# Expert rows: store by slot and gather twice, or add into x3 by an indirect DMA

## The reference

```
logits = z3 @ router_w                       # 4096 x 8
gate_vals, idx = top_k(logits, 2)            # two of eight experts for each row
gates = softmax(gate_vals)
out = 0
for e in range(8):
    h = relu(z3 @ w1[e] + b1[e]) @ w2[e] + b2[e]
    y = layernorm(z3 + h, gamma[e], beta[e])
    w = sum(where(idx == e, gates, 0))
    out = out + w[:, None] * y
return x3 + out
```

## Time and profile before

| | |
|---|---|
| median of 3 runs | 3586.35 us (3580.56 to 3590.44) |
| the profiled execution | 3575.87 us, span 3574.1 us |
| mean granted TensorE clock | 0.897 |
| slot loop, from its first to its last residual add | 3125.4 to 3457.4 us |
| the rest, to the end of the span | 3457.4 to 3574.1 us |

### The profile page before, as it was taken

How to read it: one execution, slowest core, us unless ns; L and a number is a source line. 1 busy time by engine, 2 the same in 40 slices (tenths; PEclk the granted TensorE clock), 3 DMA queues, 4 the chain that set the end, 5 groups by cost and what they waited for, 6 DMA issues and landing times. The chain is left out here.

```text
span 3574.1 us, 57773 instructions
## 1 busy us (share of the span) xinstructions
PE 2822.7 (79%) x12010; PEld 1811.5 (51%) x12011; DVE 2576.7 (72%) x5150; ACT 1472.9 (41%) x4642; POOL 2200.7 (62%) x2242
## 2 busy tenths in 40 slices
PE   7898888844888888887888887866999997599960
PEld 5555555522333333334655555645787785366630
DVE  6766666625899999998888887885656552477764
ACT  6322322213565556665545454533333332144420
POOL 2477777776777777776777777752222210088866
PEclk9788888867999999998999999987999999799985
DMA  3444444444777777776777777774222222633339
GB/s 108 170 161 142 148 157 136 150 142 151 210 208 210 209 209 210 209 209 185 214 214 213 213 210 215 212 227 152 79 73 83 73 71 95 215 109 112 112 120 320
DMA packets 234218, 594.77 MB, mean 166 GB/s; under 512 B 50865, under 2 KB 59954, under 8 KB 229170
## 3 DMA queue, kind: packets, MB, share of 16 engines
q0 software_dynamic: 127104, 362.93, 35.9%
q1 hardware_dynamic: 102898, 222.79, 17.7%
q10 hardware_dynamic: 4032, 7.34, 0.6%
HBM read 500.74 MB, written 92.15 MB: 166 GB/s over the span
## 5 line engine op out<-in xcount | busy, mean ns | idle before, releaser
L1214 PE MATMUL at_bank<-product,v_hot 128*128 128x260 f32 x2432 | 629.8, 404 | 117.8 <-DVE product L970 110.9
L1168 PE MATMUL at_bank<-wide,hot_t 128*128 x1216 | 614.1, 627 | 124.6 <-ACT hot_t L1036 65.5
L803 POOL DMA_INDIRECT fetched<-t_k,at_index x608 | 581.7, 957 | 192.5 <-issue 133.7
L812 POOL DMA_INDIRECT fetched<-t_v,at_index x608 | 577.2, 949 | 197.0 <-issue 133.1
L348 POOL DMA_INDIRECT records<-staged,address x544 | 533.1, 980 | 265.0 <-issue 165.3
L1214 PEld LDWEIGHTS at_bank<-product,v_hot 128*128 128x128 f32 x2432 | 443.1, 195 | 299.0 <-issue 136.1
L886 DVE TENSOR_TENSOR product<-at_bank,fetched 128x512 f32<-128x512 f32 x608 | 413.7, 682 | 52.4 <-issue 33.6
L970 DVE TENSOR_TENSOR product<-fetched,at_turn 128x520 f32<-128x520 f32 x608 | 405.8, 689 | 62.3 <-DMA fetched<-t_v,at_index 31.2
L1168 PEld LDWEIGHTS at_bank<-wide,hot_t 128*128 128x128 f32 x1216 | 206.6, 194 | 377.7 <-issue 332.0
L617 PE MATMUL qkv_prod<-wide 128*128 128x512 f32 x768 | 378.0, 653 | 0.0
L843 DVE TENSOR_REDUCE raw_score<-product 128x7 f32<-128x448 f32 x608 | 348.2, 575 | 0.0
(11 more groups left out here) (292 smaller groups left out, 4330.2 us busy)
## 6 DMA issues: line engine op xcount, KB each, us to landing
row_bc<-in_src SPq DMA_DIRECT2D x34, 1024.0 KB, 4.7
by_slot<-m_y SPq DMA_DIRECT2D x72, 256.0 KB, 2.0
low_bc<-low_row SPq DMA_DIRECT2D x34, 512.0 KB, 5.5
fetched<-t_k,at_index POOLq DMA_INDIRECT x608, 3.7
fetched<-t_v,at_index POOLq DMA_INDIRECT x608, 3.8
records<-staged,address POOLq DMA_INDIRECT x544, 2.1
t_v<-wide SPq DMA_DIRECT2D x32, 260.0 KB
wide<-in_x SPq DMA_DIRECT2D x32, 256.0 KB, 2.9
```

Source lines behind the costliest of these rows:

```text
L803: eng.indirect_dma_start(fetched[:, n % SLOTS, 0:C], None, k, bass.IndirectOffsetOnAxis(index[:, t:t + 1], 0)).then_inc(s_row[n % SLOTS], 16)
L812: eng.indirect_dma_start(fetched[:, n % SLOTS, :], None, v, bass.IndirectOffsetOnAxis(index[:, t:t + 1], 0)).then_inc(s_row[n % SLOTS], 16)
L1168: nc.tensor.matmul(q_edge[u % 4][:, :], hot_t[:, g % 2, u % BATCH * P:(u % BATCH + 1) * P], q_sb[:, bass.ds(at, 1), :].rearrange("p a c -> ...
L1214: last = nc.tensor.matmul(bank[g % 2 * 2 + n][:, 0:HALF], hot[:, u % 4, :], product[:, u % 4, n * HALF:(n + 1) * HALF], start=first, stop= ...
```

## The change

Each expert's tile is multiplied by its gates and added in DRAM to the rows of x3 by an indirect DMA with an add. When all is added, x3 is copied to the output. In parts:

- `by_slot`, `acc`, the 64 gathers, the loads of x3, the 64 multiply-adds and the stores of the sum are gone. SP waits for the last adds and issues 16 copies, DRAM to DRAM, of 256 rows each.
- The add of slot u-1 is issued by GpSimd at the end of slot u, from `y`, and waits until the add of slot u-2 has landed, since two tiles can hold the same row. Its indices are copied once in four slots (`put_index`).
- GpSimd's multiplication by gamma goes. VectorE does (y - mean) * gamma and then * root + beta, in two instructions of three operands in place of L2031 and L2037.
- ScalarE multiplies by the gate (`weigh`). The gate comes with the gathered row: z3 gets 8 more columns, one for each expert, and 128 rows of zeros ahead of it, for empty places. x3 gets 128 spare rows ahead of it as well. An empty place p names spare row p.
- SP stores the zero rows and the gates (4096 pieces of 32 bytes) to z3; GpSimd waits for both ahead of the first gather. VectorE makes the table of gates ahead of the lists.

```
-            def store(i, more):
-                for u in range(TURN):
-                    e_done.wait(eng, i, u)
-                    eng.dma_start(tile_rows(by_slot, i, TURN, u), y[:, u % 4, :]).then_inc(e_put.sem(u), 16)
...
+            eng.wait_ge(s_blank, 1)
+            eng.dma_start(z3[0:P, :], blank_row[:, :]).then_inc(s_gates_put, 16)
+            eng.wait_ge(s_gates, 1)
+            eng.dma_start(z3_gates, gate_of[:, 0, :, :]).then_inc(s_gates_put, 16)
+            for u in range(TURN - PUTS, TURN):
+                wait_put(eng, TURNS - 1, u)
+            for n in range(PARTS):
+                mine = slice(n * (NODES // PARTS), (n + 1) * (NODES // PARTS))
+                eng.dma_start(out[mine, :], x3[P:, :][mine, :]).then_inc(s_out, 16)
+            eng.wait_ge(s_out, 16 * PARTS)
...
+            def scatter(i, u):
+                half = u // HALF
+                wait_put(eng, i, u - 1)
+                if u % HALF == 0:
+                    eng.sem_inc(s_passed, 1)
+                    eng.tensor_copy(put_index[:, half, :], row_of[:, bass.ds(i * TURN + half * HALF, HALF)]
+                                    ).then_inc(e_put_index.sem(half), 1)
+                    e_put_index.wait(eng, i, half)
+                e_done.wait(eng, i, u)
+                eng.sem_inc(s_passed, 1)
+                eng.indirect_dma_start(x3, bass.IndirectOffsetOnAxis(put_index[:, half, u % HALF:u % HALF + 1], 0),
+                                       y[:, u % PUTS, :], None, compute_op=ALU.add).then_inc(put[u % PUTS], 16)
...
                     if u < TURN - 1 or more:
                         residual(i, u + 1)
-                    e = expert(eng, i, u)
-                    e_norm.wait(eng, i, u)
-                    eng.tensor_tensor(y[:, u % 4, :], y[:, u % 4, :], flat(gamma_sb[:, e, :]),
-                                      ALU.mult).then_inc(e_gain.sem(u), 1)
+                    if u:
+                        scatter(i, u - 1)
+                scatter(i, TURN - 1)
...
+            def weigh(i, u):
+                e = eng.value_load(expert_of[0:1, bass.ds(i * TURN + u, 1)], min_val=0, max_val=E - 1)
+                e_norm.wait(eng, i, u)
+                mine = y[:, u % PUTS, :]
+                nc.scalar.activation(mine, mine, ACT.Copy, scale=rows_sb[:, u, bass.ds(e + C, 1)]
+                                     ).then_inc(e_done.sem(u), 1)
...
                         hidden(i, u + 1)
                         hidden_columns(i, u + 1)
+                    if u:
+                        weigh(i, u - 1)
                     e_var.wait(eng, i, u)
                     nc.scalar.activation(root[:, :], mean_var[:, 1:2], ACT.Sqrt, bias=eps[:, :]).then_inc(e_root.sem(u), 1)
...
-                e_put.wait(eng, i, u - 4)
+                wait_put(eng, i, u - PUTS)
...
-                per.link(nc.vector.reciprocal(root[:, :], root[:, :]))
-                nc.vector.tensor_scalar(mine, mine, mean_var[:, 0:1], root[:, :], ALU.subtract, ALU.mult
-                                        ).then_inc(e_norm.sem(u), 1)
+                nc.vector.reciprocal(root[:, :], root[:, :])
+                per.link(nc.vector.scalar_tensor_tensor(mine, mine, mean_var[:, 0:1], flat(gamma_sb[:, e, :]),
+                                                        ALU.subtract, ALU.mult))
+                nc.vector.scalar_tensor_tensor(mine, mine, root[:, :], flat(beta_sb[:, e, :]), ALU.mult, ALU.add
+                                               ).then_inc(e_norm.sem(u), 1)
```

More of the change, by code:

```diff
@@ L1616, in _, with experts @@
             turns(begin, body, lambda t, c: (up(t), down(t, 0), down(t, 1)), eng)
-def experts(nc, moved, count, x3, z3, router, w1, b1, w2, b2, gamma, beta, by_slot, out):
+def experts(nc, moved, count, x3, z3, router, w1, b1, w2, b2, gamma, beta, out):
     EPS = 1e-6
@@ L1663, in experts @@
         row_id = sb("row_id", [P, T])
+        to_spare = sb("to_spare", [P, 1])
+        spare = sb("spare", [P, SLOTS])
         slot_at = sb("slot_at", [1, SLOTS])
-        rows_sb = sb("rows", [P, TURN, C])
+        blank_row = sb("blank_row", [P, C + E])
+        rows_sb = sb("rows", [P, TURN, C + E])
         zT = sb("zT", [P, 2, C])
@@ L1713, in experts @@
         s_both, s_counted, s_open, s_list, s_ready = (sem(n) for n in ("both", "counted", "open", "list", "ready"))
-        s_norm, s_passed, s_passed_v, s_passed_pe, s_sum = (sem(n) for n in ("norm", "passed", "passed_v", "passed_pe", "sum"))
+        s_norm, s_passed, s_passed_v, s_passed_pe = (sem(n) for n in ("norm", "passed", "passed_v", "passed_pe"))
+        s_gates, s_gates_put, s_blank, s_out = (sem(n) for n in ("gates", "gates_put", "blank", "out"))
         r_load = Ring([sem(f"load{b}") for b in range(TURN)], TURN, 16)
@@ L1723, in experts @@
         names = ("e_turn", "e_zT", "e_up", "e_h", "e_hturn", "e_hT", "e_down", "e_res", "e_y", "e_var", "e_root",
[L1724 to L1728, removed]
+                 "e_norm", "e_done")
+        (e_turn, e_zT, e_up, e_h, e_hturn, e_hT, e_down, e_res, e_y, e_var, e_root, e_norm, e_done) = (
+            Ring([sem(n)], TURN) for n in names)
+        e_index, e_put_index = (Ring([sem(n)], 2) for n in ("e_index", "e_put_index"))
         got = moved[16:16 + TURN]
-        got_y = moved[24:24 + TOP * HALF]
-        c_index, c_sum = Ring([sem("c_index")], 2), Ring([sem("c_sum")], HALF)
-        c_x3, c_out = (Ring([sem(f"{n}{b}") for b in range(HALF)], HALF, 16) for n in ("c_x3", "c_out"))
+        put = moved[16 + TURN:16 + TURN + PUTS]
         block = open_block(nc, ctx, used)
@@ L1738, in tile_rows, with wait_put @@
             return v[bass.ds(i * per + u, 1), :, :].rearrange("a p c -> (a p) c")
+        def wait_put(eng, i, u):
+            eng.wait_ge(put[u % PUTS], i * (16 * (TURN // PUTS)) + (count + 16 * (u // PUTS + 1)))
         def by_turn(eng, turns, body):
@@ L1789, in _ @@
+            for u in range(TURN - PUTS, TURN):
[4 more added lines that the diff above has]
+            eng.wait_ge(s_out, 16 * PARTS)
         @block.gpsimd
         def _(eng):
-            for r in (e_res, e_gain):
-                r.start(eng)
+            e_res.start(eng)
+            eng.memset(blank_row[:, :], 0.0).then_inc(s_blank, 1)
@@ L1815, in gather @@
                 e_res.wait(eng, i, u - TURN)
+                e_done.wait(eng, i, u - TURN)
                 eng.sem_inc(s_passed, 1)
@@ L1853, in _ @@
             by_turn(eng, TURNS, body)
[L1855 to L1872, removed]
         @block.scalar
         def _(eng):
-            for r in (r_zT, e_zT, e_h, e_hT):
+            for r in (r_zT, e_zT, e_h, e_hT, e_done):
                 r.start(eng)
-            eng.wait_ge(s_cut, 9)
+            eng.wait_ge(s_cut, 10)
             with eng.Fori(0, T // TURN) as i:
@@ L1922, in body @@
                         hidden_columns(i, u + 1)
+                    if u:
+                        weigh(i, u - 1)
                     e_var.wait(eng, i, u)
                     nc.scalar.activation(root[:, :], mean_var[:, 1:2], ACT.Sqrt, bias=eps[:, :]).then_inc(e_root.sem(u), 1)
+                weigh(i, TURN - 1)
             e_root.start(eng)
             by_turn(eng, TURNS, body)
[L1928 to L1931, removed]
         @block.vector
         def _(eng):
-            for r in (r_route_sb, r_kept, r_hot, e_y, e_var, e_norm, e_done, c_sum):
+            for r in (r_route_sb, r_kept, r_hot, e_y, e_var, e_norm):
                 r.start(eng)
@@ L1998, in _ @@
             st.link(nc.vector.tensor_tensor(gate[:, 1, :], gate[:, 0, :], ratio[:, :], ALU.mult))
+            st.link(nc.vector.tensor_tensor(gate_of[:, :, :, :], one[:, :, :, :],
+                                            gate[:, :, :].unsqueeze(3).broadcast_to([P, TOP, T, E]), ALU.mult))
+            nc.vector.tensor_tensor(gate_of[:, 0, :, :], gate_of[:, 0, :, :], gate_of[:, 1, :, :], ALU.add
+                                    ).then_inc(s_gates, 1)
             with eng.Fori(0, LIST_TURNS) as i:
@@ L2014, in _ @@
             eng.wait_ge(s_open, 2)
-            nc.vector.tensor_copy(row_of[:, :], list_ps).then_inc(s_ready, 1)
+            st.link(nc.vector.tensor_scalar(spare[:, :], list_ps, 0.0, to_spare[:, :], ALU.is_equal, ALU.mult))
+            nc.vector.scalar_tensor_tensor(row_of[:, :], list_ps, float(P - 1), spare[:, :], ALU.add, ALU.add
+                                           ).then_inc(s_ready, 1)
             eng.wait_ge(s_w, 96)
@@ L2042, in _ @@
                     norm(i, u)
[L2043 to L2053, removed]
-                                                            acc[:, u, :], ALU.mult, ALU.add))
-                    nc.vector.scalar_tensor_tensor(acc[:, u, :], rows_sb[:, u * TOP + 1, :], gate[:, 1, n],
-                                                   acc[:, u, :], ALU.mult, ALU.add).then_inc(c_sum.sem(u), 1)
         @block.tensor
```

55 lines of the change are left out of this document (23 added, 32 removed).

## The result

The changed kernel takes 3635.34 us (median of 4 runs, 3630.24 to 3647.68) against 3585.17 us; the ratio is 1.0145 (95% interval 1.0114 to 1.0175). It is 50 us slower where 75 us faster was forecast. The ratios in this document compare only the undisturbed executions of both kernels, the medians all of them. The profiled execution took 3647.68 us with a span of 3646.0 us.

What follows compares the result with a forecast made beforehand. TensorE and the ring of VectorE and GpSimd, nearly level, were taken to bound the loop, transfers the sum. Sum's removal -70, loop -7, start +1.5 on 3575.9 gave 3500 us, as median 3511; range 3480 to 3610.

Steps and rivals of the forecast that it cites:

- first two rivals: Loop: adds set the pace; first, L = 4.8, 3569 us, chance 0.17; second, up to L = 5.5, 3620 us, chance 0.20.
- second rival: Loop: adds so long that the loop eats the whole saving; at L = 5.5, +34 us, 3620 us, chance 0.20.
- turning point: Loop: the pace of 5.64 us a slot, L = 5.06, at which the loop eats the whole saving of 68.5 us.
- L: Loop and end: time from issue to landing of one indirect add to x3, taken as 4.0 us.
- the prediction's own formula: Loop: change is 71 x (pace - 4.68) us; the pace is the slowest of 4.4, 4.4 (TensorE) and L + 0.58.
- the pace of the chain of adds: Loop: each add waits for the previous landing; L plus gap 0.3 plus index copies 0.28, so 4.58 us a slot.
- The gap behind a landing: Loop: time ahead of each DMA on GpSimd, put at 0.3 us in the chain of adds.
- GpSimd's own pace: Loop: gather 1.00, residual 1.28, add issue 1.00, gaps and index copies: 4.4 us a slot; 4.9 with a dearer issue.
- costs nothing in the ordinary slot: Loop: port lock between VectorE's new instructions and GpSimd's residual; 0 in ordinary slots, up to 1.3 us with an index copy.
- the ring of VectorE and GpSimd: Loop: GpSimd at 4.69 us a slot, nearly level with TensorE's 4.4; relieving one gives 0.2 or 0.3 us at most.
- T: End: the last residual add, from which the end is counted; last add lands at T+10, kernel ends at T+47.
- The lower bound: End: the copy from DRAM to DRAM takes at least 29.9 us, as a load of 8192 KB; 36 was taken.

Runs made afterwards that it cites:

- e2: The changed kernel with a plain indirect store in place of the indirect add, all waits kept; loop 345.6 us, ratio 0.9880.
- e3: The changed kernel with each turn's last add and last weighing moved into the next turn's first slot; loop 411.4 us, ratio 1.0114.
- e6: e3's kernel with the index copy moved ahead of the wait for the add before; loop 401.5 us, ratio 1.0108 to the kernel before.
- e7: The edits of e3 and e1 together on the changed kernel, odd slots' part left out of the output; loop 363.7 us, ratio 0.9930.
- e1: The changed kernel with odd slots' adds to a second DRAM tensor, each add waiting for the one two slots before; loop 374.3 us, ratio 1.0032.
- e11: The kernel before with only the new normalising, e5's kernel on another chip; loop 298.7 us, 3548.26 us, ratio 0.9894.
- e5: The kernel before with gamma and beta in VectorE's two three-operand instructions, store by slot and sum kept; loop 298.9 us, ratio 0.9902.
- e8: The changed kernel with SP storing weighed rows by slot in place of GpSimd's add, experts' part left out of the output; loop 325.3 us, ratio 0.9836.
- e4: The kernel before with the sum replaced by the copy of x3, experts' part left out of the output; end 38.0 us for 116.7, ratio 0.9937.
- e12: e6's kernel timed again on the chip of e11, against the kernel before; loop 401.3 us, 3595.27 us, ratio 1.0025.

## Why the prediction was wrong

That the adds set the pace was in the forecast itself and in its first two rivals, at different lengths. By the sign the second rival came, with a chance of 0.20; by the length of an add it is not, since its turning point was put at L = 5.06, and L is 4.9. By the prediction's own formula the kernel should still have been some 10 us faster. So more than one step failed, and that a rival named the right sign is in part luck. The steps that failed are the pace of the chain of adds, put at L + 0.58 = 4.58 (points 1 and 2), and the ends of the turns, put at nothing (point 3).

1. **The length of an add** (the term of the sum that was mis-sized): L = 4.0 was taken between 3.5 and 5.5; 4.9 was measured. The base was right: an indirect store without the add was put at 2.7 and takes 2.9 to 3.2 (e2), 0.2 to 0.5 more. The add's own part was put at 1.3 and is 1.8. That is 0.9 x 71 = 64 us. The Trainium skill's rule of two reads for each write ("Collectives: The Full Stack", bandwidth ceiling), stated there for a ring of cores, gave 3.6 as an estimate; the measured add costs 1.8 us over the store, twice what doubling the 0.93 us of data would cost. The rule points the right way and is too small here.
2. **The gap behind a landing**: 0.3 was taken from DMAs issued back to back. Behind a wait it is 0.8 (e2, and the chain after). Those 0.5 us, 36 us in 71 slots, turn the sign once L is 4.9: 10 us faster become 26 slower. A row of issues that wait for nothing doesn't price an issue that waits.
3. **The ends of the turns** were not in the sum at all. The diff shows `scatter(i, TURN - 1)` behind the loop over u; the prediction treated every slot alike. 32 us (e3), the add's place and the weighing's together. With the three put right, and 0.14 us a slot for the index copies (e3 to e6), the formula gives 71 x (4.9 + 0.8 + 0.14 - 4.68) + 32 = 114 us for the loop; 112 were measured.
4. **GpSimd's own pace** was put at 4.4, with an add's issue at 1.0. It is 5.1 (e7), with 1.7 to 1.8 for the issue there and 1.6 in the kernel after. The upper bound named for it was 1.5.
5. **VectorE against GpSimd**: "costs nothing in the ordinary slot" held for a GpSimd that arrives when computed. In e1 and e7, where it has hardly a pause, the instruction with gamma takes 1.29 and 1.48 for 0.76, in the kernel after 0.90. The exclusive lock of the Trainium skill's "SBUF — State Buffer" fits.
6. **The new normalising** was worth nothing in the prediction, TensorE standing at 4.4 a slot. Alone it is worth 33 us. TensorE's 318 us of busy time were no floor: between the first and the last residual add the same number of its instructions was busy 308.7 us before and 292.9 in e11, which runs at 4.2 a slot. Busy time read in a loop that waits can be too long. The kernel before was bound by the ring of VectorE and GpSimd, and by more than 0.3 us.
7. **The end** came out at 47.2 for 47, with errors that cancel: the copy starts at T+17.7 for T+10, and takes 29.5 for 36. The later start comes from a third add still outstanding at T: they were issued at T+1.0, T+6.7 and T+12.9 (3599.82, 3605.49, 3611.74), where the sum had two, at T+1.7 and T+6.0. The lower bound, a load of the same size in 29.9 us, was the right row for a copy from DRAM to DRAM.
8. **The start**: +1.5 was right for the lists (+1.0); the gates' store landed 7.4 us after its issue, at 3118.0, well ahead of the first gather at 3137.6. Routing and fill were 6.9 us longer than in the trace before, which is within their scatter.

The loop's +112 us, from kernel to kernel: the new normalising -33 (before to e5), the weighing, at the turns' ends, +26 (e5 to e8), GpSimd's issuing of stores with its waits +20 (e8 to e2), and the add in place of the store +98 (e2 to after). These runs don't split the 98 cleanly. e7, which keeps the add without the chain and without the ends, lies 80 below the kernel after and 18 above e2; but e2 still waits for its own stores (27.6 us) and has its own ends.

The removal of the sum (e4, 79 us) and the new normalising (e5, 33 us in the loop) were tried alone. Adding in DRAM was not tried without the new normalising; with it, it costs more than the sum's removal gives (e12 against e11). The version that beats both kernels is e11's: store by slot and sum as before, gamma and beta in VectorE's two instructions, 3548 us.

## What to carry to other kernels

When transfers must follow one another, price the whole period, landing plus the way from the landing to the next issue, and compare it with the loop's pace before any saving elsewhere: here 5.7 against 4.7 us, paid 72 times. A chain shows as a loop in which no engine is full. Read the order at the loop's edges as closely as its middle: here they cost twice, in the adds and in the weighing. And try each part of a change alone: here the part meant as a help was the only one worth keeping.

## What the runs showed of the hardware

- An indirect add of 128 rows of 2 KB to DRAM lands in 4.7 to 5.0 us (72 adds of the kernel after), a plain indirect store of them in 2.9 to 3.2 (four of e2's loop). The median issue holds GpSimd for 1.60 us and 1.13 us.
- From the landing of such a DMA to the start of the next one that waits for it on GpSimd it took 0.8 to 0.9 us (e2, after); DMAs that wait for nothing were 0.3 apart.
- 8.39 MB copied from DRAM to DRAM in 16 pieces take 29 to 31 us in all ten kernels that do it, 280 GB/s, as long as the load of 8192 KB in the earlier trace rows.
- 4096 pieces of 32 bytes, stored from SBUF to DRAM in one DMA, landed in 7.4 us in the kernel after, in 5.4 to 8.8 in the experiments.
- Chips can differ by 630 to 750 us in the earlier stages of this kernel and by under 1% in the loop of the last.
